# Spreading the softmax reciprocals by transfers through DRAM instead of widened transposes, in a two-layer graph network kernel on one core

## The chip, the cores and the metric

The kernel runs on one core of one Trainium2 chip. The metric is the device time of one execution in microseconds, as a median of runs. The engines of the core are TensorE (PE, with its weight loads as PEld), VectorE (DVE), ScalarE (ACT), GpSimd (POOL) and SyncE (SP); each works through its own list of instructions in order, and semaphores connect them.

## The reference

Sixteen graphs of 512 nodes with 512 features go through two layers. The first picks one of four expert matrices for each graph, multiplies by the adjacency matrix and applies a batch normalisation and a ReLU; the second, which the change touches, is an attention with 16 heads of 32 columns and the adjacency matrix as a bias:

```python
x = _layernorm(x + L0(x, adj, ...))
a = jnp.einsum('bhnd,bhmd->bhnm', q, k) * scale + (adj + adj)[:, None]
row_nonzero = jnp.any(a != 0, axis=-1, keepdims=True)
a = jnp.where(row_nonzero, a, -jnp.inf)
p = jax.nn.softmax(a, axis=-1)
p = jnp.where(jnp.isnan(p), 0.0, p)
o = jnp.einsum('bhnm,bhmd->bhnd', p, v)          # B=16, H=16 heads, N=512, hd=32
x = _layernorm(x + o.transpose(0, 2, 1, 3).reshape(B, N, D) @ Wo.T)
```

All of it is float32. Large products are made of three products of rounded high and low parts.

## The kernel before, in words

Layer 0 runs first, over all 16 graphs; layer 1 follows, from about 400 us on, and is written out for every batch `b` (one graph). A batch has 16 steps `s`. Four steps make a group `g` of four heads; step `s` handles rows `t = s % 4` (128 of them) of the four heads of group `s // 4`. Each engine has its own order of the work of a step, written out by hand in its function `batch`, and the batches overlap: the projections of the next batch and the output projection of the one before fill the slots between the attention steps.

In step `s` PE makes the scores of step `s+1` (`scores`, line 630, four heads), one dense slot of 12 matmuls (line 615, from the list `SLOTS`), the transposes of the probabilities of step `s` (`prob_transpose`, line 661), and in every second step the products of the transposed probabilities with `v` (`weigh_v`, line 645). DVE adds the bias to the scores and takes row maxima (`bias_and_max`, line 1175), ACT takes the exponential with its row sum (`exp`, line 881) and copies the transposed probabilities out of PSUM (`copy_probT`, line 781; the fourth head is copied by DVE in most steps, line 1189).

When a group's four steps are through, its 16 x 128 row sums have to divide the product. The result of a group lies in `pv_bank` with partition = head and column, free dimension = row n, while the row sums lie with the row n on the partition. So in the last step of a group, DVE forms `inv_sum` and `zeros_inv` (`inverse_sum`), POOL subtracts them and repeats each value 32 times (`recip_wide`, [128, 16, 32], line 479), and in the first step of the next group (`s % 4 == 0`) PE transposes the four 128 x 128 blocks of it (`spread_recip`, line 653) into `t_bank[0]`. ACT copies the bank to `recip` (`copy_recip`), DVE multiplies `pv_bank` by it (`weigh`, line 1205, the last or nearly the last thing that DVE does in that step, waiting for `r_sb` and `pv_ps`), and ACT and DVE split the result into its high and low parts (`oT_high`, `oT_low`) at the steps in `OT_STEPS`: group 0 in step 6, group 1 in step 8, group 2 in step 12, group 3 in step 0 of the next batch. For groups 1, 2 and 3 that is the very step of the `weigh`. On ACT, `oT_high` stands after the first two `copy_probT` and ahead of the exponentials of the next step.

POOL also forms the reciprocal standard deviations of both layer norms (`layer_norm_rstd`), stores the outputs (`store_out`, line 486) and loads the next batch's x (`load_x`, line 494) over the tile of z that a store has freed. SP issues all else: above all `pack`, which moves the staged q and k into the layout of the scores, 1 MB for each slot of kind k or q (line 386), the adjacency rows (line 371), layer 0's output (line 375) and the copies of x1 to DRAM and back.

Of the kernel before, what the change touches and what calls it, by code (L numbers as in the profile page):

```python
# [41 lines left out]
         + [("o", 0, -1), ("o", 1, -1), ("o", 2, -1), ("q", 2, 0), ("o", 3, -1), ("k", 3, 0), ("q", 3, 0)]  # L42
# [5 lines left out]
X_LOADS = {2: 0, 4: 1, 5: 2, 6: 3}  # L48
# [7 lines left out]
OT_STEPS = {0: 3, 6: 0, 8: 1, 12: 2}  # L56
# [47 lines left out]
def gnn_program(nc, x, adj, adj_t, router_wt, router_b, expert_w, bn_gamma, bn_beta, WqT, WkT, WvT, WoT, out):  # L104
    outT_dram = nc.dram_tensor("outT_spill", [B, H, N], F32).ap()
    x1_dram = nc.dram_tensor("x1_spill", [B, N, H], F32).ap()

# [8 lines left out]
    with ExitStack() as ctx:  # L116
# [56 lines left out]
        with ExitStack() as l1:  # L173
# [12 lines left out]
            recip_wide = sb(l1, "recip_wide", [P, NT * J, HD])  # L186
# [81 lines left out]
        r_sb = sem("r_sb")  # L268
        o_norm = sem("o_norm")
# [162 lines left out]
        def _(pool):  # L432
# [29 lines left out]
            def softmax_weights(b, g):  # L462
# [15 lines left out]
                wide = [P, NT * J, HD]  # L478
                nc.gpsimd.tensor_tensor(recip_wide[:, :, :],
                                        inv_sum[:, :].rearrange("p (a o) -> p a o", o=1).broadcast_to(wide),  # L480
                                        zeros_inv[:, :].rearrange("p (a o) -> p a o", o=1).broadcast_to(wide),
                                        ALU.subtract).then_inc(wide_done, 1)

# [18 lines left out]
            def batch(b, par, first, last):  # L502
                for s in range(STEPS):
                    if s in X_LOADS and not last:
                        load_x(b + 1, X_LOADS[s], first)
# [9 lines left out]
            iterations(batch)  # L515
            for t in range(NT):
                layer_norm_rstd(1, B - 1, t, f_mv, f_eps, f_rstd)
# [5 lines left out]
        def _(pe):  # L523
# [125 lines left out]
            def spread_recip(b, g):  # L649

                pe.wait_ge(wide_done, G * b + g + 1)
                for t in range(NT):
                    ins = nc.tensor.transpose(t_bank[0][:, t * P:(t + 1) * P],  # L653
                                              recip_wide[:, J * t:J * t + J, :].rearrange("p a d -> p (a d)"),
                                              ident[:, :])
                ins.then_inc(r_ps, 1)
# [122 lines left out]
        def _(act):  # L779
# [109 lines left out]
            def copy_recip(b, g):  # L889
                act.wait_ge(r_ps, G * b + g + 1)  # L890
                need(act, oT_lo, G * b + g)
                copy(recip[:, :], t_bank[0][:, :]).then_inc(r_sb, 1)
# [17 lines left out]
            def batch(b, par, first, last):  # L910
                for s in range(STEPS):
# [6 lines left out]
                    if s in XT_EARLY and not last:  # L918
                        xT_high(b + 1, XT_EARLY[s], xT_bank[XT_EARLY[s]])
                    copy_probT(b, s, 0)  # L920
                    copy_probT(b, s, 1)
                    if s in OT_STEPS and not (first and s == 0):
                        oT_high(b if s else b - 1, OT_STEPS[s])
# [411 lines left out]
```

## Time and profile before

| | before |
|---|---|
| median of 3 runs | 2219.53 us (2218.31 to 2220.68) |
| profiled execution | 2221.48 us, its span 2219.7 us |
| PE busy | 2126.9 us, 96% of the span |
| DVE busy | 1584.6 us, 71% |
| ACT busy | 1567.1 us, 71% |
| POOL busy | 302.7 us, 14% |
| mean granted clock of PE | 0.989 |
| moved by DMA | 297.18 MB, 134 GB/s over the span |

Busy times are of one profiled execution. PE counts as busy while a matmul is in its pipeline; issuing a DMA, waiting and branching are not counted. A timeline row gives the start, the duration, the engine, the line and operation, what is written from what, how many were merged, and in brackets the idle time ahead of it with the instruction that ended it. The layers' two parts look different: layer 1 repeats every 110.8 us, one batch, which is the distance of the `weigh_v` rows of step 12 in successive batches (1301.26 us and 1412.06 us in the chain of work that ended last).

### The profile page before, as it was taken

The page shows a single profiled execution, that of the slowest core. Times are in us where ns is not written, and L with a number is a line of the kernel's source. Part 1 is how long each engine was busy: PE and PEld are TensorE (multiplying, and loading weights), DVE is VectorE, ACT ScalarE, POOL GpSimd, SP SyncE. Part 2 cuts the span into 40 slices and gives each one's busy share as a digit, 9 for nine tenths or more (in the row PEclk, how much of TensorE's full clock was granted, in tenths as well). Part 3 has the DMA queues.
Part 4 walks back from the last instruction along what each step waited for, and adds up shares of the span by engine and source line. Part 5 has one row for each costly group of instructions (what it writes and reads, how often), then busy time and mean ns, then how long its engine had stood idle before and what let it go on. Part 6 is the DMA issues. An engine that isn't in the chain of part 4 may idle for free.

```text
span 2219.7 us, 42446 instructions
## 1 busy us (share of the span) xinstructions
PE 2126.9 (96%) x14627; PEld 1685.1 (76%) x14627; DVE 1584.6 (71%) x4020; ACT 1567.1 (71%) x3501; POOL 302.7 (14%) x659
## 2 busy tenths in 40 slices
PE   6999999689999999999999999999999999999996
PEld 5778887467777777777777777777777777777774
DVE  5887877366768686868686868686868686868675
ACT  3544443287878787878787878787878787878784
POOL 0000000110202020202020202020202020202011
PEclk9999999799999999999999999999999999999999
DMA  6444342687777777777777777777778777877761
GB/s 225 158 162 155 124 159 85 121 143 129 138 133 134 134 135 132 136 130 138 135 132 134 134 134 134 132 136 130 135 132 136 134 134 130 136 134 133 132 100 45
DMA packets 149008, 297.18 MB, mean 134 GB/s; under 512 B 14514, under 2 KB 14546, under 8 KB 148690
## 3 DMA queue, kind: packets, MB, share of 16 engines
q1 hardware_dynamic: 137490, 256.97, 61.7%
q0 software_dynamic: 11328, 37.76, 6.1%
q8 instruction: 110, 1.80, 0.4%
q14 instruction: 80, 0.66, 0.1%
HBM read 110.12 MB, written 50.33 MB: 72 GB/s over the span
## 4 chain that ended last, share of the span: by engine, by line
PE 71%; issue 13%; DVE 7%; ACT 7%; DMA 1%; POOL 0%; SPq 0%; DVEq 0%; ACTq 0%; POOLq 0%
PE bank L615 27%; PE bank L661 18%; PE bank L645 11%; PE bank L630 8%; ACT prob L881 3%; DVE prob L1175 3%; PE bank L535 2%; ACT probT L781 2%; PE bank L552 2%; PE bank L587 1%; PE bank L653 1%; DVE z L1140 1%; DVE st_ln L1133 1%; DVE probT L1189 1%; DMA qp<-stage_q 1%
## 5 line engine op out<-in xcount | busy, mean ns | idle before, releaser
L1175 DVE CUSTOM_DVE_ANT_0 prob<-bank,adj_sb 128x512 f32<-128x512 f32 x1024 | 657.6, 685 | 141.0 <-PE bank L630 141.0
L881 ACT ACTIVATE prob<-prob,neg_max 128x512 f32<-128x512 f32 x1024 | 731.4, 723 | 9.4 <-DVE neg_max L1184 5.5
L781 ACT ACTIVATE probT<-bank 128x512 f32<-128x512 f32 x824 | 455.6, 594 | 321.1 <-PE bank L661 318.7
L661 PEld LDWEIGHTS bank<-ident,prob 128*128 128x128 f32 x4096 | 463.8, 140 | 110.6 <-issue 51.9
L661 PE MATMUL bank<-ident,prob 128*128 128x128 f32 x4096 | 541.0, 275 | 4.6 <-ACT probT L781 3.1
L630 PE MATMUL bank<-kp,qp 128*128 128x512 f32 x1024 | 347.3, 420 | 24.7 <-DVE row_max L1175 23.5
L1189 DVE COPY probT<-bank 128x512 f32<-128x512 f32 x200 | 136.4, 685 | 232.4 <-PE bank L661 232.4
L645 PE MATMUL bank<-probT,v 128*32 128x256 f32 x4096 | 247.6, 382 | 0.8 <-issue 0.8
L630 PEld LDWEIGHTS bank<-kp,qp 128*128 128x128 f32 x1024 | 175.9, 189 | 57.7 <-DVE row_max L1175 35.7
L615 PE MATMUL bank<-xT,wkT 128*128 128x512 f32 x768 | 205.3, 404 | 1.5 <-DVE xT L954 1.5
L881 ACT ACTIVATION_READ_ACCUMULATOR prob<-prob,neg_max 128x1 f32 x1024 | 204.4, 200 | 0.0
L615 PE MATMUL bank<-woT,oT 128*128 128x512 f32 x768 | 202.0, 399 | 0.0
L615 PE MATMUL bank<-xT,wqT 128*128 128x512 f32 x768 | 201.7, 398 | 0.0
L645 PEld LDWEIGHTS bank<-probT,v 128*32 128x32 f32 x4096 | 120.3, 109 | 104.3 <-issue 38.7
L535 PE MATMUL bank<-adjT,x_part 128*128 128x512 f32 x768 | 184.7, 397 | 13.1 <-DVE adjT L967 13.1
L615 PE MATMUL bank<-wvT,xT 128*128 128x512 f32 x768 | 196.2, 398 | 0.0
L552 PE MATMUL bank<-zT,w_sel 128*128 128x512 f32 x768 | 180.4, 393 | 8.4 <-ACT outT L781 5.2
L535 PEld LDWEIGHTS bank<-adjT,x_part 128*128 128x128 f32 x768 | 145.1, 191 | 43.7 <-issue 13.1
L552 PEld LDWEIGHTS bank<-zT,w_sel 128*128 128x128 f32 x768 | 144.7, 189 | 41.7 <-ACT outT L781 7.3
L615 PEld LDWEIGHTS bank<-xT,wkT 128*128 128x128 f32 x768 | 142.0, 192 | 29.7 <-issue 1.9
L615 PEld LDWEIGHTS bank<-woT,oT 128*128 128x128 f32 x768 | 139.4, 188 | 27.9 <-DVE oT L954 0.4
L615 PEld LDWEIGHTS bank<-wvT,xT 128*128 128x128 f32 x768 | 139.7, 188 | 27.5
(112 smaller groups left out, 2091.5 us busy)
## 6 DMA issues: line engine op xcount, KB each, us to landing
kp<-stage_k SPq DMA_DIRECT2D x256, 256.0 KB, 6.9
qp<-stage_q SPq DMA_DIRECT2D x256, 256.0 KB, 8.5
x_raw<-in_x_dram SPq DMA_DIRECT2D x16, 1024.0 KB, 7.5
adj_raw<-in_adj_t_dram SPq DMA_DIRECT2D x16, 1024.0 KB, 9.6
outT_spill<-outT SPq DMA_DIRECT2D x16, 1024.0 KB, 5.1
v<-outT_spill SPq DMA_DIRECT2D x16, 1024.0 KB, 15.1
z<-in_x_dram POOLq DMA_DIRECT2D x64, 256.0 KB, 3.9
adj_sb<-in_adj_dram SPq DMA_DIRECT2D x64, 256.0 KB, 8.2
```

Of the source, the lines that this page charges most:

```text
L535: ins = mm(z_bank[i][:, :], x_part[a][:, mt, i * P:(i + 1) * P], adjT[c][:, mt, :], start=(mt == 0 and n == 0), stop=(mt == NT - 1 and n = ...
L552: ins = mm(ps[:, :], w_sel[a][:, ht, i * P:(i + 1) * P], zT[c][:, ht, :], start=(ht == 0 and n == 0), stop=(ht == NT - 1 and n == 2))
L587: ins = nc.tensor.transpose(ps[:, kt * P:(kt + 1) * P], v[:, par, kt, t * P:(t + 1) * P], ident[:, :])
L615: ins = mm(ps[:, :], w, m, start=(t == 0 and n == 0), stop=(t == NT - 1 and n == 2))
L630: mm(s_bank[j][:, :], qp[:, g % 2, j, t * P:(t + 1) * P], kp[:, g % 2, j, :], start=True, stop=True).then_inc(s_ps, 1)
L645: ins = mm(pv_bank[j * HD:(j + 1) * HD, (t - 1) * P:(t + 1) * P], v[:, par, mt, c:c + HD], probT[:, j, mt, :], start=(mt == 0), stop=(mt = ...
L653: ins = nc.tensor.transpose(t_bank[0][:, t * P:(t + 1) * P], recip_wide[:, J * t:J * t + J, :].rearrange("p a d -> p (a d)"), ident[:, :])
L661: ins = nc.tensor.transpose(t_bank[j % 2][:, mt * P:(mt + 1) * P], prob[:, s % 2, j, mt * P:(mt + 1) * P], ident[:, :])
L781: return nc.scalar.activation(dst, src, ACT.Copy, scale=scale)
L881: nc.scalar.activation(prob[:, s % 2, j, :], prob[:, s % 2, j, :], ACT.Exp, scale=2.0, bias=neg_max[:, s % 2, j:j + 1], accum_out=row_sum[ ...
L1175: nc.vector.tensor_tensor_reduce(prob[:, s % 2, j, :], s_bank[j][:, :], adj_sb[:, t, :], 1.0, LOWEST, ALU.add, ALU.max, row_max[:, g % 2, ...
L1189: nc.vector.tensor_copy(probT[:, j, :, s % 2 * P:(s % 2 + 1) * P], by_block(t_bank[j % 2])).then_inc(pT_dve, 1)
```

## The change

The widened transposes go. POOL subtracts only the 16 columns (`inv_live`, [128, 16]), PE transposes them with one instruction to [16, 128], ACT copies these 16 rows to `recip_rows`, and a new function `spread_rows` on the POOL queue stores them to a scratch tensor in DRAM (8 KB), waits for that to land, and loads for each of the four heads one row of 512 values into 32 partitions of `recip` (64 KB each). `weigh` now waits for these four loads in place of ACT's copy. `spread_rows` stands first in POOL's steps 0, 4, 8 and 12. The high and low parts of group 3 move from step 0 to step 1 of the next batch; to suit that, the slots of the output projection move one later (2, 3, 4, 5 instead of 1, 2, 3, 5) and the q slot of group 2 from 4 to 1; the x loads of tiles 1 to 3 move from steps 4, 5, 6 to 5, 6, 7.

```diff
 SLOTS = ([("k", 2, 0)]
-         + [("o", 0, -1), ("o", 1, -1), ("o", 2, -1), ("q", 2, 0), ("o", 3, -1), ("k", 3, 0), ("q", 3, 0)]
+         + [("q", 2, 0), ("o", 0, -1), ("o", 1, -1), ("o", 2, -1), ("o", 3, -1), ("k", 3, 0), ("q", 3, 0)]
-X_LOADS = {2: 0, 4: 1, 5: 2, 6: 3}
+X_LOADS = {2: 0, 5: 1, 6: 2, 7: 3}
-OT_STEPS = {0: 3, 6: 0, 8: 1, 12: 2}
+OT_STEPS = {6: 0, 8: 1, 12: 2}
+OT_LAST = 1
+    recip_dram = nc.dram_tensor("recip_spill", [B * G, J, N], F32).ap()
-            recip_wide = sb(l1, "recip_wide", [P, NT * J, HD])
+            inv_live = sb(l1, "inv_live", [P, NT * J])
+            recip_rows = sb(l1, "recip_rows", [NT * J, P])
...
-                nc.gpsimd.tensor_tensor(recip_wide[:, :, :],
-                                        inv_sum[:, :].rearrange("p (a o) -> p a o", o=1).broadcast_to(wide),
-                                        zeros_inv[:, :].rearrange("p (a o) -> p a o", o=1).broadcast_to(wide),
+                nc.gpsimd.tensor_tensor(inv_live[:, :], inv_sum[:, :], zeros_inv[:, :],
                                         ALU.subtract).then_inc(wide_done, 1)
+            def spread_rows(b, g):
+                n = G * b + g
+                pool.wait_ge(r_sb, n + 1)
+                pool.dma_start(recip_dram[n:n + 1, :, :].rearrange("o j (t n) -> t (o j) n", n=P),
+                               recip_rows[:, :]).then_inc(recip_out, 16)
+                need(pool, oT_lo, n)
+                pool.wait_ge(recip_out, 16 * n + 16)
+                for j in range(J):
+                    pool.dma_start(recip[j * HD:(j + 1) * HD, :],
+                                   recip_dram[n:n + 1, j, :].broadcast_to([HD, N])).then_inc(recip_in, 16)
...
                 for s in range(STEPS):
+                    if s % NT == 0 and s > 0:
+                        spread_rows(b, s // NT - 1)
+                    elif s == 0 and not first:
+                        spread_rows(b - 1, G - 1)
                     if s in X_LOADS and not last:
...
-                for t in range(NT):
-                    ins = nc.tensor.transpose(t_bank[0][:, t * P:(t + 1) * P],
-                                              recip_wide[:, J * t:J * t + J, :].rearrange("p a d -> p (a d)"),
-                                              ident[:, :])
-                ins.then_inc(r_ps, 1)
+                nc.tensor.transpose(t_bank[0][0:NT * J, 0:P], inv_live[:, :], ident[:, :]).then_inc(r_ps, 1)
...
-                need(act, oT_lo, G * b + g)
-                copy(recip[:, :], t_bank[0][:, :]).then_inc(r_sb, 1)
+                need(act, recip_out, 16 * (G * b + g))
+                copy(recip_rows[:, :], t_bank[0][0:NT * J, 0:P]).then_inc(r_sb, 1)
...
+                    if s == OT_LAST and not first:
+                        oT_high(b - 1, G - 1)
                     copy_probT(b, s, 0)
                     copy_probT(b, s, 1)
-                    if s in OT_STEPS and not (first and s == 0):
-                        oT_high(b if s else b - 1, OT_STEPS[s])
+                    if s in OT_STEPS:
+                        oT_high(b, OT_STEPS[s])
...
-                dve.wait_ge(r_sb, G * b + g + 1)
+                dve.wait_ge(recip_in, 64 * (G * b + g + 1))
                 dve.wait_ge(pv_ps, 8 * b + 2 * g + 2)
                 tt(recip[:, :], pv_bank[:, :], recip[:, :], ALU.mult).then_inc(o_norm, 1)
...
                         bias_and_max(nb, ns, (0, 1, 2))
+                    if s == OT_LAST and not first:
+                        oT_low(b - 1, G - 1)
...
                         weigh(gb, gg)
-                    if s == 0 and not first:
-                        oT_low(b - 1, OT_STEPS[s])
```

## Rows read from the trace of the kernel before

**Rows 1.** The page: busy time of PE, and the chain's shares by engine
```profile
PE 2126.9 (96%) x14627; PEld 1685.1 (76%) x14627; DVE 1584.6 (71%) x4020; ACT 1567.1 (71%) x3501; POOL 302.7 (14%) x659
...
PE 71%; issue 13%; DVE 7%; ACT 7%; DMA 1%; POOL 0%; SPq 0%; DVEq 0%; ACTq 0%; POOLq 0%
```

**Rows 2.** Windows: stretch: length, busy us by engine, granted clock, DMA share, GB/s
```profile
1299.70:1306.30 6.60, 6.60 (x64) 4.90 (x64) 3.46 (x11) 4.19 (x11) 0.00 (x0) 1.00 0.94 128
...
1325.00:1332.50 7.50, 7.50 (x68) 5.66 (x67) 5.03 (x13) 5.37 (x13) 0.46 (x1) 1.00 1.08 184
...
1352.00:1358.70 6.70, 6.70 (x65) 5.01 (x64) 5.04 (x14) 5.10 (x12) 3.92 (x8) 1.00 0.23 78
...
1378.80:1389.00 10.20, 9.20 (x79) 6.94 (x78) 8.91 (x21) 6.83 (x16) 3.02 (x6) 1.00 1.08 156
```

**Rows 3.** Timeline of step 12 of one batch, from the transposes on
```profile
1300.20 0.59 PEld L653 LDWEIGHTS bank<-ident,recip_wide 128*128 128x128 f32 x4
...
1301.06 0.60 ACT L781 ACTIVATE recip<-bank 128x512 f32<-128x512 f32 x1 [0.32 <-PE bank L653]
...
1303.27 0.69 DVE L1205 TENSOR_TENSOR recip<-bank,recip 128x512 f32<-128x512 f32 x1 [0.76 <-PE bank L645]
...
1304.72 0.63 ACT L781 ACTIVATE oT<-recip 128x512 fp32r<-128x512 f32 x1
...
1306.65 0.59 ACT L781 ACTIVATE probT<-bank 128x512 f32<-128x512 f32 x1
...
1308.58 1.03 PE L661 MATMUL bank<-ident,prob 128*128 128x128 f32 x8
```

**Rows 4.** Timeline of steps 0 and 1 of the next batch
```profile
1327.24 0.60 ACT L781 ACTIVATE recip<-bank 128x512 f32<-128x512 f32 x1
...
1332.64 0.69 DVE L1189 COPY probT<-bank 128x512 f32<-128x512 f32 x1 [0.38 <-PE bank L661]
...
1333.25 0.68 DVE L1175 CUSTOM_DVE_ANT_0 prob<-bank,adj_sb 128x512 f32<-128x512 f32 x1
...
1334.52 0.39 PE L630 MATMUL bank<-kp,qp 128*128 128x512 f32 x1
```

**Rows 5.** Timeline of steps 4 and 5 of that batch
```profile
1353.92 0.59 ACT L781 ACTIVATE recip<-bank 128x512 f32<-128x512 f32 x1
...
1359.17 0.69 DVE L1175 CUSTOM_DVE_ANT_0 prob<-bank,adj_sb 128x512 f32<-128x512 f32 x1 [2.04 <-PE bank L630]
...
1360.69 0.39 PE L630 MATMUL bank<-kp,qp 128*128 128x512 f32 x1
```

**Rows 6.** Timeline of steps 8 and 9 of that batch
```profile
1380.95 0.59 ACT L781 ACTIVATE recip<-bank 128x512 f32<-128x512 f32 x1
...
1385.68 0.68 DVE L1148 TENSOR_TENSOR z<-bank,z 128x512 f32<-128x512 f32 x1
...
1389.49 0.69 DVE L1175 CUSTOM_DVE_ANT_0 prob<-bank,adj_sb 128x512 f32<-128x512 f32 x1 [1.61 <-PE bank L630]
...
1390.24 0.50 PE L630 MATMUL bank<-kp,qp 128*128 128x512 f32 x1
```

**Rows 7.** Groups of POOL: the widening, and the issue of a 256 KB store
```profile
L479 POOL TENSOR_TENSOR recip_wide<-inv_sum,zeros_inv 128x512 f32<-128x512 f32 x64 | 72.2, 1129 | 110.0 <-issue 96.6 <-POOL live L473 12.9 <-DVE zeros_inv L1199 0.5
L486 POOL DMA_DIRECT2D out_dram<-z x64 | 39.1, 612 | 36.8 <-DVE z L1140 34.5 <-issue 2.2
```

**Rows 8.** Issue to landing, POOL queue: all stores of 256 KB (line 486)
```profile
DMA to landing us min/median/max: 2.4/3.2/9.6
```

**Rows 9.** The same: loads of 256 KB (line 494), all; the one at 1324.8 us
```profile
DMA to landing us min/median/max: 2.8/4.2/11.6
...
DMA to landing us min/median/max: 8.1/8.1/8.1
```

**Rows 10.** Windows of the first layer and of the start of layer 1
```profile
30.00:35.00 5.00, 2.66 (x8) 2.13 (x9) 5.00 (x3) 3.92 (x3) 0.00 (x0) 0.84 0.00 0
...
440.00:445.00 5.00, 2.79 (x7) 2.03 (x8) 4.41 (x15) 2.10 (x6) 0.00 (x0) 0.80 1.09 129
```

More of the change, by code:

```diff
@@ L268, in gnn_program @@
         r_sb = sem("r_sb")
+        recip_out = sem("recip_out")
+        recip_in = sem("recip_in")
         o_norm = sem("o_norm")
@@ L477, in softmax_weights @@
                 wait_apart(pool, r_ps, G * b + g)
-                wide = [P, NT * J, HD]
-                nc.gpsimd.tensor_tensor(recip_wide[:, :, :],
-                                        inv_sum[:, :].rearrange("p (a o) -> p a o", o=1).broadcast_to(wide),
-                                        zeros_inv[:, :].rearrange("p (a o) -> p a o", o=1).broadcast_to(wide),
+                nc.gpsimd.tensor_tensor(inv_live[:, :], inv_sum[:, :], zeros_inv[:, :],
                                         ALU.subtract).then_inc(wide_done, 1)
+            def spread_rows(b, g):
[8 more added lines that the diff above has]
+                                   recip_dram[n:n + 1, j, :].broadcast_to([HD, N])).then_inc(recip_in, 16)
             def store_out(b, t):
@@ L515, in _ @@
             iterations(batch)
+            spread_rows(B - 1, G - 1)
             for t in range(NT):
```

## The prediction

> **What bounds the kernel now.** I read the page first, then windows over one batch of layer 1, then the timeline around each of its four hand-overs of the reciprocals, and last how long the POOL queue's transfers take. The page shows PE busy 96% of the span and 71% of the chain on PE [rows 1]. In windows around three of the four hand-overs PE is busy for the whole stretch, and for 9.20 of 10.20 us in the fourth, at a granted clock of 1.00 [rows 2]. So PE sets the pace, nearly without gaps: a microsecond taken off PE comes off the time, and any wait that PE meets for longer than the slack of the engine that feeds it goes on top. The other column to see is the DMA share: 0.94 in step 12, 1.08 in step 0, 1.08 in step 8, but 0.23 in step 4. Three of the four places where the change wants a fast transfer have full DMA engines.
>
> **What is taken away.** PE loses three of four transposes. Four weight loads, which pace them, take 0.59 us [rows 3], so three are 0.44 us; 64 groups give 28 us, all on PE's path. The remaining transpose has only 16 columns of weights and can only be cheaper. ACT's copy of 128x512 (0.60 us) becomes one of 16x128, for which I take 0.25 us (no row shows it; it is between nothing and 0.6 us); ACT isn't the bound there, and the gain is counted below as an earlier start. POOL's 1.13 us becomes a 16-column subtraction, at most as long [rows 7]; POOL is 14% busy and works ahead, so it is worth nothing.
>
> **What is added: a round trip T** from the end of the small copy to the landing of the last of the four loads, ahead of DVE's `weigh`. It is one store, its landing, four issues in a row and the last one's landing. An issue holds POOL 0.61 us [rows 7]; I take 0.6. From issue to landing a 256 KB store takes 2.4 us at best [rows 8] and a 256 KB load 2.8 us [rows 9]. With these T = 2.4 + 3 x 0.6 + 2.8 = 7.0 us on idle DMA engines. The transfers here are smaller (8 KB, and 64 KB four times), which takes off some of the data's part; five issues alone are 3.0 us, which is the floor. I take 6.3, nearer to the 7.0 since most of a short transfer's landing doesn't look like data. On full engines the load issued at 1324.8 us took 8.1 us [rows 9] and the slowest store 9.6 us [rows 8]: T could be up to 9.6 + 1.8 + 8.1 = 19.5 us. The new transfers have fewer packets to be held up, so I stay near the low end: 8.5 us in steps 0 and 12, 7.5 in step 8, 6.3 in step 4.
>
> The Trainium skill (DMA: Bandwidth & Descriptors, Anatomy of one DMA — SWDGE (gpsimd) path) fits such a transfer as about 2.0 us plus its bytes at 436 GB/s. For 256 KB that estimate is 2.6 us, and the best rows, 2.4 and 2.8, agree. For this change it would give 2.0 + 1.8 + 2.15 = 6.0 us in an estimate, which is the second rival's value, at every group.
>
> **What T costs, group by group.** What waits is in-order, so everything behind it shifts.
> Step 12: the small copy ends at about 1301.0 (the old one began at 1301.06 after a wait of 0.32 for the four transposes). `weigh` would end at 1301.7 + T; it takes 0.69. Behind it in the same step waits ACT's `oT_high`, which began at 1304.72, and behind that on ACT are two exponentials and the copy of the third head's transposed probabilities, 1306.65 to 1307.24. PE wants that bank for the transposes recorded at 1308.58, loading weights from about 1308.35: 1.1 us of slack. PE's wait is T - 3.0 - 1.1 = T - 4.1 [rows 3]; at 8.5, 4.4 us.
> Step 0: the copy ends at 1327.5, `weigh` at 1328.2 + T. Here `oT_high` has been moved to step 1, so ACT doesn't wait at once; but DVE does, and its next work began at 1332.64, then the maxima at 1333.25, which end 0.5 us ahead of the scores at 1334.52 that need their bank. PE's wait is T - 4.4 - 0.5 = T - 4.9 [rows 4]; at 8.5, 3.6 us.
> Step 4: copy until 1354.2, `weigh` until 1354.9 + T; DVE's next work was at 1359.17 after 2.04 us of idling, 0.8 us ahead of PE's need at 1360.69. PE's wait is T - 5.1 [rows 5]; at 6.3, 1.2 us.
> Step 8: copy until 1381.2, `weigh` until 1381.9 + T; next on DVE is the sum for the next batch's x at 1385.68, its statistics and a copy, then 1.61 us idle, then the maximum at 1389.49, for which PE's scores at 1390.24 wait without slack. PE's wait is T - 3.8 - 1.6 = T - 5.4 [rows 6]; at 7.5, 2.1 us. `oT_high` stands in this step too, and gives a little less.
> The wait on DVE and the one on ACT run side by side, so the larger counts. Steps 4, 8 and 12 come 16 times and step 0 15 times: 16 x (1.2 + 2.1 + 4.4) + 15 x 3.6 = 123 + 54 = 177 us. At the very end the last `weigh` stands bare, but PE has other output products; I put 4 us.
>
> **Edits that I cost at nothing.** The slots are exchanged, not added: PE has 12 matmuls in each either way. DVE's work for the output projection (sum and statistics, about 1.6 us) leaves step 2 and comes to step 5, where DVE is loaded; the idle time at steps 5 to 8 is what hides it, and if `weigh` has used that up it is 0.9 us more in each batch, 14 us. The x loads are one step later, each behind a store issued one step later; `spread_rows` also holds POOL for T less the last landing, some 4 to 6 us, ahead of the stores, the layer norm's rstd and the loads. The loads are wanted at the end of steps 6 to 8, 10 us after their issue, against 4.2 us in the median and 11.6 at worst [rows 9]. The group-3 parts are one step later and so are the slots that read them. Of the DMA bytes, 264 KB are added to each group.
>
> **The sum**, against the profiled execution's 2221.5 us: 2221.5 - 28 + 177 + 4 = 2374.5 us. It is 2 us above the median of the runs, so I forecast 2373 us.
>
> **Rivals.**
> *The round trip is hidden (faster).* If T stays under the 4.1 to 5.4 us of slack at every group, only the 28 us are left: 2192 us. That needs each landing within about 1.2 us after its issue ends (5.3 less five issues, halved). For it: no transfer as small as these stands in the trace. Against it: 2.4 us is the minimum of 64 stores. It turns at a mean wait of 0.44 us, T of about 5.3. Chance 0.08 for a gain, 0.03 for a draw.
> *Traffic doesn't matter, T is about 6 everywhere.* The waits are 1.9, 1.1, 0.9 and 0.6 us: 16 x 3.4 + 15 x 1.1 + 3 - 28 = +46 us, 2266 us. For it: an engine may take turns between queues packet by packet, and these transfers give each only one or two packets at a time. The Trainium skill (DMA: Bandwidth & Descriptors, Queues, rings and completion order) says that it does so. Against it: the 8.1 us load in a full stretch has eight packets an engine and yet 5.3 us more than the quickest. Chance 0.24.
> *Worse in traffic, or the clock falls.* With T of 12 in steps 0 and 12 and 10 in step 8 the waits are 7.9, 7.1, 4.6 and 1.2: +302 us, 2521 us. Besides, where PE was busy for only 2.66 and 2.79 of 5 us the granted clock was 0.84 and 0.80 [rows 10], that is part of the stretch at the lower of the levels 2.4 and 1.2 GHz; 0.20 of 5 us is 1 us for each long wait, 31 of them, 31 us on any of the cases. Chance 0.20.
> *The x chain.* If store and load are both slow (over 15 us in all), the sum for x at steps 6 to 8 waits on DVE; 2 to 3 us in a batch, 40 us more on the forecast. Chance 0.05, inside the range.
>
> **Numbers.** The forecast has 0.40, its worse neighbours 0.25, the 6 us case 0.24, the hidden case 0.11. The range leaves out the gain and the draw and most of what lies over T = 12: 2235 to 2500 us. A measurement of this kernel tells 0.2%, about 4 us, from no change. Faster 0.08, same 0.03, slower 0.89.
>
> **What would show it.** In the profile after: idle time of DVE ahead of line 1205's `weigh` put down to a DMA of `recip`, several microseconds each, where it idled 0.76 us by PE in step 12 [rows 3]; one transpose in place of four; POOL issues at 0.6 us; PE idle ahead of scores or transposes in steps 1, 5, 9 and 13; the landing of the four loads shorter in step 4 than in steps 0 and 12. The forecast is wrong if the round trip is under 5.3 us, or if ACT and DVE win back in the steps between what they lose; it is then PE's share of the chain that stays above 70%.

## The result and the profile after

| | before | after |
|---|---|---|
| median | 2219.56 us | 2848.95 us (2842.78 to 2849.55, 4 runs) |
| ratio | | 1.283, 95% interval 1.281 to 1.284 |
| span of the profiled execution | 2219.7 us | 2846.9 us |
| PE busy / not busy in the span | 2126.9 / 92.8 us | 2268.8 / 578.1 us |
| mean granted clock | 0.989 | 0.893 |

Slower, as forecast, but by 629 us where 153 were forecast. The page of the kernel after, in the form of [rows 1]: busy time, granted clock in tenths along the span, the chain by engine and by line.

```profile
PE 2268.8 (80%) x14435; PEld 1780.7 (63%) x14435; DVE 1583.1 (56%) x4020; ACT 1553.1 (55%) x3501; POOL 425.7 (15%) x979
...
PEclk9999989889898988888998888888989888889888
...
PE 37%; DMA 24%; issue 14%; DVE 10%; ACT 10%; POOL 4%; SPq 0%; DVEq 0%; POOLq 0%; ACTq 0%
DMA recip_spill<-recip_rows 16%; PE bank L634 13%; PE bank L676 10%; DMA recip<-recip_spill 7%; ACT prob L896 5%; DVE prob L1192 4%; PE bank L649 4%; PE bank L664 4%; POOL recip L495 3%; ACT probT L796 2%; PE bank L554 2%; PE bank L571 1%; DVE st_ln L1150 1%; ACT v L870 1%; PE bank L606 1%
```

PE's share of the chain fell from 71% to 37%, and a transfer of 8 KB (`recip_spill`) now holds 16% of it, more than any matmul line. Who waited for whom (total, times, longest, in us):

```profile
DVE recip L1222 <- DMA recip<-recip_spill: 669.7, 64, 16.2
...
ACT oT L796 <- DVE recip L1222: 451.0, 48, 14.6
POOL recip L495 <- DMA recip_spill<-recip_rows: 444.4, 64, 10.4
...
PE bank L649 <- DVE row_max L1192: 389.7, 86, 15.0
```

That is the chain that the prediction named: POOL waits for its store, DVE's `weigh` for the loads, ACT's `oT_high` for `weigh`, PE's scores for DVE. The timeline of step 0 of one batch, the place of [rows 4]:

```profile
1630.98 0.25 ACT L796 ACTIVATE recip_rows<-bank 16x128 f32<-16x128 f32 x1
...
1631.52 0.63 POOL L490 DMA_DIRECT2D recip_spill<-recip_rows  x1 [3.58 <-ACT recip_rows L796]
...
1641.24 1.97 POOL L495 DMA_DIRECT2D recip<-recip_spill  x4 [9.09 <-DMA recip_spill<-recip_rows]
...
1647.51 0.69 DVE L1222 TENSOR_TENSOR recip<-bank,recip 128x512 f32<-128x512 f32 x1 [14.95 <-DMA recip<-recip_spill]
...
1649.46 0.80 PE L649 MATMUL bank<-kp,qp 128*128 128x512 f32 x1 [11.23 <-DVE row_max L1192]
```

The round trip T, from the end of the small copy (1631.23) to the start of `weigh`, is 16.3 us: 0.3 until POOL issues, 9.2 until the store of 8 KB has landed, 0.5 until the first load is issued, 1.5 for three more issues, and 4.8 for the last landing. PE waits 11.23 us for scores. Times from issue to landing over the whole execution, first the 64 stores of 8 KB, then the 256 loads of 64 KB (min, median, max), as in [rows 8, 9]:

```profile
DMA to landing us min/median/max: 1.8/6.0/10.5
...
DMA to landing us min/median/max: 2.1/2.5/6.1
```

Taken from the timeline as above for the inner 14 batches, the medians of T in steps 4, 8, 12 and 0 are 10.2, 14.0, 10.5 and 16.4 us. Between one group's small copy and the next PE idles 5.1, 9.9, 6.0 and 11.3 us, as means over all groups; the last batch's step 8 alone has 17.4 us, and without it the 9.9 are 9.4. (The kernel before idles 1.3 us in step 4 and next to nothing in the others.) The forecast had 1.2, 2.1, 4.4 and 3.6 us: it is 1.4 times too short in step 12 and three to five times in the others.

The last two stores of the execution, where SP has no packs in flight, took 1.8 us each. The other 62 were issued while transfers of SP were under way. Each landed between 0.4 us before and 1.5 us after the last one of SP's that had been issued ahead of it (medians 1.1, 0.5, 0.4 and 0.4 us after it, in the order of the steps). So the store of 8 KB comes in as if it stood in line behind them. Part of the delay passes before its data move: the first of its packets starts 5.9 us after the issue in step 0 and 2.7 us in steps 4 and 12 (medians), 1.3 us in the quiet store.

The clock, in windows of 10 us around the end of two such waits (PE had idled 11.2 us until 1649.46 and 7.9 us until 1570.04; length, busy us of PE, PEld, DVE, ACT, POOL, granted clock, DMA share, GB/s), to be set beside the 1.00 of [rows 2]:

```profile
1646.00:1656.00 10.00, 6.54 (x31) 5.73 (x32) 6.20 (x16) 5.14 (x11) 0.00 (x0) 0.68 0.08 21
1569.00:1579.00 10.00, 7.95 (x33) 7.04 (x34) 8.17 (x19) 8.37 (x20) 0.79 (x2) 0.58 0.27 101
```

A mean of 0.58 between the levels 1.0 (2.4 GHz) and 0.5 (1.2 GHz) is most of 10 us at the lower level. Over the whole span the granted clock is at 0.5 for 607 us, mostly 6.8 to 13.7 us at a time around the waits, and PE is busy in 346 us of them; in the kernel before it is 50 us, PE busy in 24.

**Where the time went.** The span grew by 627.2 us: 485.3 of PE not busy and 141.9 of PE busy. PE has 28 us less to do, so its matmuls took some 170 us more, 2.7 us a group. That is what the clock explains: half of the 346 us that PE was busy at the lower level is 173 us, 12 us in the kernel before. Both parts come from the same 64 waits.

### The profile page after: what moved, and what is told of

It reads as the page before. It is cut to its first block, busy times and chain, and to the rows that moved or that the text cites. A ratio compares the mean times of both kernels' runs of the same rounds, so it can differ in the third digit from the quotient of the medians.

```text
span 2846.9 us, 42445 instructions
## 1 busy us (share of the span) xinstructions
PE 2268.8 (80%) x14435; PEld 1780.7 (63%) x14435; DVE 1583.1 (56%) x4020; ACT 1553.1 (55%) x3501; POOL 425.7 (15%) x979
## 4 chain that ended last, share of the span: by engine, by line
PE 37%; DMA 24%; issue 14%; DVE 10%; ACT 10%; POOL 4%; SPq 0%; DVEq 0%; POOLq 0%; ACTq 0%
DMA recip_spill<-recip_rows 16%; PE bank L634 13%; PE bank L676 10%; DMA recip<-recip_spill 7%; ACT prob L896 5%; DVE prob L1192 4%; PE bank L649 4%; PE bank L664 4%; POOL recip L495 3%; ACT probT L796 2%; PE bank L554 2%; PE bank L571 1%; DVE st_ln L1150 1%; ACT v L870 1%; PE bank L606 1%
## 5 line engine op out<-in xcount | busy, mean ns | idle before, releaser
L649 PE MATMUL bank<-kp,qp 128*128 128x512 f32 x1024 | 371.0, 444 | 390.5 <-DVE row_max L1192 389.7
L676 PE MATMUL bank<-ident,prob 128*128 128x128 f32 x4096 | 613.0, 299 | 12.1 <-ACT probT L796 11.7
L676 PEld LDWEIGHTS bank<-ident,prob 128*128 128x128 f32 x4096 | 531.4, 155 | 126.8 <-issue 65.4
L1222 DVE TENSOR_TENSOR recip<-bank,recip 128x512 f32<-128x512 f32 x64 | 44.2, 691 | 669.7 <-DMA recip<-recip_spill 669.7
L796 ACT ACTIVATE oT<-recip 128x512 fp32r<-128x512 f32 x64 | 40.3, 630 | 451.0 <-DVE recip L1222 451.0
L634 PE MATMUL bank<-woT,oT 128*128 128x512 f32 x768 | 217.0, 421 | 4.1 <-DVE oT L971 4.1
L634 PE MATMUL bank<-xT,wqT 128*128 128x512 f32 x768 | 217.4, 422 | 0.0
L634 PE MATMUL bank<-wvT,xT 128*128 128x512 f32 x768 | 215.0, 426 | 0.0
L495 POOL DMA_DIRECT2D recip<-recip_spill x256 | 127.1, 503 | 451.9 <-DMA recip_spill<-recip_rows 444.4
L554 PE MATMUL bank<-adjT,x_part 128*128 128x512 f32 x768 | 183.3, 395 | 13.7 <-DVE adjT L984 13.7
L634 PEld LDWEIGHTS bank<-wvT,xT 128*128 128x128 f32 x768 | 153.0, 207 | 30.6
## 6 DMA issues: line engine op xcount, KB each, us to landing
v<-outT_spill SPq DMA_DIRECT2D x16, 1024.0 KB, 13.6
```

What stands on the lines that cost most here:

```text
L495: pool.dma_start(recip[j * HD:(j + 1) * HD, :], recip_dram[n:n + 1, j, :].broadcast_to([HD, N])).then_inc(recip_in, 16)
L554: ins = mm(z_bank[i][:, :], x_part[a][:, mt, i * P:(i + 1) * P], adjT[c][:, mt, :], start=(mt == 0 and n == 0), stop=(mt == NT - 1 and n = ...
L634: ins = mm(ps[:, :], w, m, start=(t == 0 and n == 0), stop=(t == NT - 1 and n == 2))
L649: mm(s_bank[j][:, :], qp[:, g % 2, j, t * P:(t + 1) * P], kp[:, g % 2, j, :], start=True, stop=True).then_inc(s_ps, 1)
L676: ins = nc.tensor.transpose(t_bank[j % 2][:, mt * P:(mt + 1) * P], prob[:, s % 2, j, mt * P:(mt + 1) * P], ident[:, :])
L796: return nc.scalar.activation(dst, src, ACT.Copy, scale=scale)
```

## The experiments

All are against the kernel before on the same chip, which took 2219.6 to 2221.3 us each time. Where T and idle times are given by step, they are medians (T) and means over all groups (idle) read from the timeline as above, in the order 4, 8, 12, 0.

**1. The moves alone.** The kernel before with the changed lists and the later high and low parts of group 3, on the old path by four transposes.

```diff
-         + [("o", 0, -1), ("o", 1, -1), ("o", 2, -1), ("q", 2, 0), ("o", 3, -1), ("k", 3, 0), ("q", 3, 0)]
+         + [("q", 2, 0), ("o", 0, -1), ("o", 1, -1), ("o", 2, -1), ("o", 3, -1), ("k", 3, 0), ("q", 3, 0)]
-X_LOADS = {2: 0, 4: 1, 5: 2, 6: 3}
-OT_STEPS = {0: 3, 6: 0, 8: 1, 12: 2}
+X_LOADS = {2: 0, 5: 1, 6: 2, 7: 3}
+OT_STEPS = {6: 0, 8: 1, 12: 2}
+OT_LAST = 1
...
```

> The kernel before with the moves alone: the q slot of group 2 to slot 1, the output projection to slots 2 to 5, the x loads of tiles 1 to 3 to steps 5 to 7, the high and low parts of group 3 to step 1. The reciprocals still go by four transposes. My theory (the moves are worth next to nothing, all of the loss is the new round trip and what follows from it): 2220 us, within 15 us. Rival (the moves take DVE's and POOL's slack in steps 5 to 8 and are a good part of the 629 us): 2300 us or more, with idle time of PE ahead of the transposes or scores of steps 5 to 9.

Measured: 2227.5 us, ratio 1.0032 (1.0018 to 1.0046). The moves cost 7 us; the other 622 are the path of the reciprocals.

**2. Stale rows: loads that needn't wait for the store.**

```diff
-                pool.wait_ge(recip_out, 16 * n + 16)
+                old = max(n - 1, 0)
+                pool.wait_ge(recip_out, 16 * old + 16)
                 for j in range(J):
                     pool.dma_start(recip[j * HD:(j + 1) * HD, :],
-                                   recip_dram[n:n + 1, j, :].broadcast_to([HD, N])).then_inc(recip_in, 16)
+                                   recip_dram[old:old + 1, j, :].broadcast_to([HD, N])).then_inc(recip_in, 16)
```

> The changed kernel, but the four loads read the rows of the group before in DRAM (so the reciprocals are those of another group) and so needn't wait for this group's store to land; everything else, the store too, stays. Theory 1 (what is slow is a write to DRAM and its receipt, 5 to 10 us of each round trip, and loads on the same queue aren't held up): the round trip is 0.65 + 1.5 + 2.2 to 4.8 us, 4.4 to 7 us; PE's waits nearly go and the time is 2250 to 2350 us. Theory 2 (a short transfer of any kind issued while SP's pack transfers are in flight waits behind them): the loads land as late as store and loads did before less 2 us, 7 to 11 us after their issue in steps 0 and 8, and the time stays over 2600 us.

Measured: 2730.3 us, ratio 1.230. The loads' landings and DVE's wait:

```profile
DMA to landing us min/median/max: 2.1/7.5/12.2
...
DVE recip L1223 <- DMA recip<-recip_spill: 546.9, 64, 13.2
```

The same loads that took 2.5 us in the median now take 7.5: the waiting that the store had done ahead of them they do themselves. So it isn't only the write to DRAM that is slow; loads issued into the same traffic wait as long. T is 6.5, 12.2, 10.7 and 13.4 us.

**3. Thin packs.** From the third group on, each of SP's pack transfers moves 32 of 128 rows (the scores use stale rows).

```diff
-                        sp.dma_start(f32(dst[part * HD:(part + 1) * HD, ring, :, :]).rearrange("p j n -> p (j n)"),
-                                     f32(stage[m][half][:, :])).then_inc(packed[m], 16)
+                        rows_moved = HD if b == 0 and g < 2 else HD // 4
+                        sp.dma_start(f32(dst[part * HD:part * HD + rows_moved, ring, :, :]).rearrange("p j n -> p (j n)"),
+                                     f32(stage[m][half][0:J * rows_moved, :])).then_inc(packed[m], 16)
```

> The changed kernel, but from the third group on each of SP's q and k pack transfers moves 32 of its 128 rows (64 KB in place of 256 KB; the scores use stale rows). Same count of transfers. Theory 1 (a store to DRAM is slow by itself): the stores land as before, median 6 us, up to 10 us; the time stays within 10% of 2849 us. Theory 2 (the wait is behind the pack transfers): the stores land in 1.8 to 3 us and the loads in 2.1 to 2.5 us, the round trip is about 6 us, and the time falls to 2250 to 2400 us. The last two stores of the changed kernel, with no pack beside them, landed in 1.8 us.

Measured: 2506.2 us, ratio 1.129; the stores', then the loads' landings, and DVE's wait:

```profile
DMA to landing us min/median/max: 1.7/2.5/4.2
...
DMA to landing us min/median/max: 2.1/2.2/4.4
...
DVE recip L1223 <- DMA recip<-recip_spill: 360.5, 64, 8.8
```

Taking bytes away from another queue brings the 8 KB store from 6.0 to 2.5 us. T is 6.2, 8.2, 7.1 and 9.5 us. The time was 106 us over the upper end expected: even this T is beyond the slack in every step, and PE not busy is 300.0 us (2510.2 span less 2210.2 busy), 207 over before, with 111 us of slow matmuls on top (2210.2 less 2126.9, plus 28).

**4. The same thin packs in the kernel before,** a control.

> A control: the kernel before with the thin packs (32 of 128 rows from the third group on). Both theories want it to be at 2215 to 2222 us, since PE doesn't wait for packs there. If it is much faster, part of what thin packs gained in the changed kernel was not the round trip.

Measured: 2217.5 us, ratio 0.9988 (0.9978 to 0.9998). So the 343 us that thin packs gave the changed kernel came by way of its round trips.

**5. The store issued by ACT.**

```diff
-                pool.dma_start(recip_dram[n:n + 1, :, :].rearrange("o j (t n) -> t (o j) n", n=P),
-                               recip_rows[:, :]).then_inc(recip_out, 16)
...
+                n = G * b + g
...
+                act.wait_ge(r_sb, n + 1)
+                act.dma_start(recip_dram[n:n + 1, :, :].rearrange("o j (t n) -> t (o j) n", n=P),
+                              recip_rows[:, :]).then_inc(recip_out, 16)
```

> The changed kernel, but the 8 KB store is issued by ACT right behind its small copy; the loads stay on POOL. Theory 1 (the POOL queue is what is slow: issue in software and a queue of its own behind its other transfers): the store lands in about 2.5 us, the time falls to 2500 us or less. Theory 2 (the DMA engines behind are shared and full of SP's packs): landing still 4 to 9 us and the time within 5% of 2849 us.

Measured: 2814.2 us, ratio 1.268. T is 8.8, 13.6, 10.5 and 16.0 us, shorter by 1.4 us at most. So it isn't the POOL queue that is slow; the traffic met the store on ACT's queue too.

**6. No trip to DRAM: rows straight from SBUF.**

```diff
-                pool.dma_start(recip_dram[n:n + 1, :, :].rearrange("o j (t n) -> t (o j) n", n=P),
-                               recip_rows[:, :]).then_inc(recip_out, 16)
-                pool.wait_ge(recip_out, 16 * n + 16)
...
-                    pool.dma_start(recip[j * HD:(j + 1) * HD, :],
-                                   recip_dram[n:n + 1, j, :].broadcast_to([HD, N])).then_inc(recip_in, 16)
+                    rows4 = recip_rows[J * j:J * j + J, :].rearrange("p (o n) -> p o n", o=1)
+                    pool.dma_start(recip[:, j * P:(j + 1) * P],
+                                   rows4.broadcast_to([J, HD, P])).then_inc(recip_in, 16)
...
```

> The changed kernel without the trip to DRAM: the four DMAs on the POOL queue take the 16 rows straight from SBUF (each four rows of 512 B, repeated over 32 partitions each), so the store and its landing are gone. Theory 1 (each transfer issued beside SP's packs waits behind them once, whatever it is): the round trip loses the quiet part of the store, about 2.5 us, and in each group keeps the wait behind the packs; with a mean of 12.7 us before, 9 to 10 us are left, and the time is 2600 to 2730 us, near the kernel with stale rows (2730 us). Theory 2 (the DRAM write is slow in itself): the round trip is 4 to 6 us and the time under 2350 us.

Measured: 2815.3 us, ratio 1.268: neither of the two. The landings of the four transfers:

```profile
DMA to landing us min/median/max: 2.7/8.6/14.0
```

T is 8.4, 15.0, 11.5 and 15.4 us. One of the two hops is gone, and T is shorter by 1.8 and 1.0 us in two steps and longer by 1.0 in the others. They now carry 512 B a packet, four times as many packets, and a longer issue (0.68 us for 0.50); which of it uses up the gain wasn't taken apart.

**7. Everything that waits, one step later** (rows by DRAM as in the change).

```diff
-OT_STEPS = {6: 0, 8: 1, 12: 2}
-OT_LAST = 1
+OT_STEPS = {6: 0, 10: 1, 13: 2}
+OT_LAST = 2
...
+                    late_end = None
+                    if s % NT == 1 and not (first and s == 1):
+                        late_end = (b, s // NT - 1) if s > 1 else (b - 1, G - 1)
...
-                    if group_end:
-                        weigh(gb, gg)
+                    if late_end:
+                        weigh(*late_end)
```

> The changed kernel with everything that waits for the round trip one step later: weigh in steps 1, 5, 9, 13 in place of 0, 4, 8, 12, the high and low parts of groups 1, 2 and 3 in steps 10, 13 and 2. That gives each group 6.8 us more slack, 10.9 to 12.2 us in all. My theory (PE waits for the round trip less the slack, 31 us a batch in the changed kernel): of the round trips of 16.3, 9.7, 15.1 and 11.0 us there are left 4.4, 0, 2.9 and 0.1 us a batch, some 7 us, 115 us in all, less 28 us saved, and some clock: 2300 to 2380 us. Rival (the engines are bound by something else that the change brought, such as POOL being held up or the added DMA traffic): over 2500 us.

Measured: 2498.0 us, ratio 1.125, between the two ranges. PE idles 0.8, 2.6, 6.0 and 5.4 us: 14.8 a batch for 32.3. Step 4 has no wait left. But the traffic's timing shifted with the rest, and T of step 12 grew from 10.5 to 16.4 us, so that step didn't gain; that is the miss. The store of step 12 still takes 4.9 us, the last of its loads 8.7 us where it had taken 3.3: in the batch looked at, two packs of slot 12 go out between the store's landing and the third load. So each hop pays for what goes out ahead of it.

**8. Both: rows from SBUF, and a step later.**

> Both: rows straight from SBUF, and everything that waits for them one step later. Round trip 9 to 10 us in the mean, 13 at most, against 10.9 to 12.2 us of slack. My theory: PE waits about 1 us a batch or less, the three transposes saved are 28 us, the moves cost 7: 2195 to 2230 us. Rival (more traffic and waits in POOL leave a part): 2250 to 2350 us.

Measured: 2380.6 us, ratio 1.070 (1.067 to 1.073), above both ranges. T is 14.8, 11.6 and 15.0 us in steps 8, 12 and 0, where 13 at most was expected, and PE idles 0.8, 2.7, 2.7 and 3.6 us.

**9. Three packs held back until the rows of a group have landed,** in the changed kernel, and (10) in the kernel of 8.

```diff
+HELD = {7: 1, 11: 2, 15: 3}
...
+                    if s in HELD and is_live(s, first, last):
+                        sp.wait_ge(recip_in, 64 * (G * b + HELD[s] + 1))
                     if kind in "kq" and is_live(s, first, last):
                         pack(kind, b + rel, i)
```

> The changed kernel with nothing but the three held packs. Its round trips are 14.0, 10.5 and 16.4 us in steps 8, 12 and 0. My theory: they fall to the 7 to 10 us seen with thin packs, step 4 stays at 10.2, and PE waits for each round trip less 4.1 to 5.4 us, 14 to 20 us a batch in place of 31: 2450 to 2600 us. Rival (not the packs issued just ahead but the queue as a whole): over 2750 us.

Measured: 2673.1 us, ratio 1.203. T is 11.0, 10.2, 6.4 and 7.5 us: in the three steps that were held it falls from 14.0, 10.5 and 16.4, in step 4, which wasn't, it doesn't (10.2 before). What is issued just ahead is what the short transfer waits behind. The time fell by 176 us only and ended 73 us above the range. Holding has a price of its own: ACT waits 41.6 us for `stage_q`, and PE 78.3 us in 15 waits for which the profile names no releaser ("issue"). In each of these 15 PE starts 0.1 us after the last pack of q slot 12 has landed, which SP had to issue behind the held one of slot 11.

> The kernel with the rows taken straight from SBUF and all that waits for them one step later, and besides SP holds back three pack transfers a batch until the loads of a group have landed: that of q slot 7 for group 1, of k slot 11 for group 2, of q slot 15 for group 3. So those 1 MB no longer lie ahead of the short transfers on the DMA engines. My theory (short transfers wait behind packs already issued): the round trips of steps 8, 12 and 0 fall from 14.8, 11.6 and 15.0 us to 7 to 10 us, less than the 11 to 12 us of slack; PE's waits go, and the time is 2195 to 2240 us. Rival (the held packs come late for the scores that need them, or the packs ahead of the held ones fill the engines all the same): round trips over 11 us in two of the steps, or PE waiting for a DMA of kp or qp, and 2300 us or more.

Measured: 2516.9 us, ratio 1.133, worse than 8 by 136 us. The rival held on the time and on the late packs. The theory held on the round trips: the last landing now comes 8.0, 7.7 and 7.8 us after the copy in steps 8, 12 and 0, where it had come at 14.7, 11.6 and 14.9. `weigh`'s wait is all but gone, and two others stand in its place:

```profile
DVE recip L1223 <- DMA recip<-recip_rows: 11.0, 3, 7.8
...
PE bank L650 <- issue: 141.9, 16, 9.7
...
ACT stage_q L797 <- DMA qp<-stage_q: 102.3, 16, 7.1
```

Slots 15 and 1 both stage through `stage_q`. And the packs of slot 12, behind the held one of slot 11, come late for the first scores of the next batch: PE starts 0.1 us after the last of them in all 16 waits.

**11. The packs moved out of the way in place of held.** From 8: k1, q1, v3 in slots 13 to 15, and only q slot 7 held.

```diff
-         + [("v", 0, 1), ("v", 1, 1), ("v", 2, 1), ("k", 0, 1), ("q", 0, 1), ("v", 3, 1), ("k", 1, 1), ("q", 1, 1)])
+         + [("v", 0, 1), ("v", 1, 1), ("v", 2, 1), ("k", 0, 1), ("q", 0, 1), ("k", 1, 1), ("q", 1, 1), ("v", 3, 1)])
...
+HELD = {7: 1}
```

> From the kernel with direct rows and late weigh: k1, q1, v3 take slots 13, 14, 15 in place of v3, k1, q1, so that q1's pack goes out one step earlier, 6.8 us ahead of the short transfers of step 0, and one pack is held (q slot 7, until group 1's rows are there); stage_q is free for its next user, 5 slots on. My theory (a round trip is the quiet 5 to 6 us plus what of the packs is still in flight, and PE waits for it less 11 to 12 us of slack): round trips of 12 us in step 8, 11.6 in step 12, 10 to 12 in step 0; PE idles 1 to 4 us a batch in all against 1.8 in the kernel before; with 28 us saved and 7 for the moves 2200 to 2250 us. Rival (the v load and adjacency loads fill the engines in step 0 as well as packs did, and held packs cost their own wait): the round trip of step 0 stays at 14 us or more, PE waits there 3 us or more, and the time is 2280 us or more.

Measured: 2350.5 us, ratio 1.058 (1.056 to 1.060), 30 us better than 8 and the fastest by this path, still 130 behind the kernel before. `weigh` in step 8 starts 12.0 us after the copy, which is where DVE comes to it, so nothing is waited for there; T of step 12 is 11.2 and of step 0 14.1 us: the rival's sign, in the stretch where 1 MB of v and the adjacency rows are loaded besides the packs; which of them sets it wasn't taken apart. PE idles 0.8, 1.6, 2.7 and 3.0 us. The span is 128 us longer than before: 104 us more of PE not busy (196.4 less 92.8) and 52 us of slow matmuls, less the 28.

**12 and 13. Needless matmuls in PE's waits,** to see what the clock is worth. First the dense slot twice more ahead of the step's last transposes:

> The changed kernel, but in the steps 0, 4, 8 and 12 PE makes the 12 matmuls of its dense slot two more times (same bank, same result), some 5 us of needless work a group, just ahead of where it waits. The changed kernel's PE is busy 142 us more than before though it has 28 us less to do, at a mean granted clock of 0.893 against 0.989. Theory 1 (the waits pull the clock down and slow matmuls are about 170 us of the 629): with PE busy most of the waits the granted clock is over 0.96 and the time falls by 60 to 150 us, to 2700 to 2790 us, though there is more to do. Theory 2 (the slow stretches lie beside work that sets nothing, and the waits alone are the loss): 2849 us or up to 100 us more.

Then behind them, 3, 1, 3 and 2 times in steps 0, 4, 8 and 12:

```diff
+AGAIN = {0: 3, 4: 1, 8: 3, 12: 2}
...
+                    if there and s in AGAIN:
+                        for n in range(AGAIN[s]):
+                            dense(kind, b + rel, i, range(NT), dense_bank[s % 2], n == AGAIN[s] - 1)
...
```

> The changed kernel with needless matmuls in PE's waits as in the other filled kernel, but put behind all transposes of the step, where nobody waits for them, and sized to the wait: the dense slot again 3, 1, 3 and 2 times in steps 0, 4, 8 and 12 (7.8, 2.6, 7.8 and 5.2 us at full clock, where PE waits 11.3, 5.1, 9.9 and 6.0 us). Theory 1 (the clock lost in the waits is about 170 us of slow matmuls, most of them on the path): granted clock over 0.96 and a time of 2700 to 2790 us. Theory 2 (slow matmuls mostly lie beside other waits): 2800 to 2880 us in spite of the clock.

Measured: 2820.2 us at a clock of 0.955, and 2821.1 us at 0.961, 29 and 28 us less than the changed kernel, with 1464 and 1656 more matmuls. The busy time of PE, first and second:

```profile
PE 2511.2 (89%) x15899; PEld 1980.1 (70%) x15899; DVE 1582.4 (56%) x4020; ACT 1553.1 (55%) x3501; POOL 426.7 (15%) x979
```

```profile
PE 2558.5 (91%) x16091; PEld 2015.9 (71%) x16091; DVE 1581.8 (56%) x4020; ACT 1550.8 (55%) x3501; POOL 426.0 (15%) x979
```

A matmul more costs about 0.23 us at full clock (a slot of 12 took 2.78 us in the chain of before). So at full clock PE would be busy 2126.9 - 28 + 337 = 2436 us and, with 381 in place of 337, 2480 us; 75 and 79 us of slow matmuls are left of 170. The granted clock agrees: PE was busy at the lower level for 145 and 148 us in place of 346. So over 90 us of slow matmuls are gone, and that gave 29 and 28 us of time. The round trips took little of it back: added up over the 64 groups, T grew by 18 and 5 us, mostly in step 0 (from 16.4 to 18.2 and 17.4 us).

So doing more work made the kernel faster, as the first theory has it, but by half of the least that it expected. The second filled kernel got the clock of the first theory (0.961) and the time of the second (2821 us). Most of the slow matmuls seem to lie beside other waits: over 90 us less of them were worth about 30 us. What all 170 would be worth stays open.

## Why the prediction was right and wrong

**Right: the chain, and what each step's slack is worth.** The prediction said that PE waits for T less 5.1, 5.4, 4.1 and 4.9 us in steps 4, 8, 12 and 0 [rows 3 to 6]. Put the measured T into it: 10.2 - 5.1 = 5.1, 14.0 - 5.4 = 8.6, 10.5 - 4.1 = 6.4, 16.4 - 4.9 = 11.5 us; measured were 5.1, 9.9 (9.4 without the last batch), 6.0 and 11.3 of idle time in all. Over the execution 16 x 20.1 + 15 x 11.5 = 494 us, against 485.3 us more than before. Single steps are off by up to about 1 us either way, so the sum's 2% is in part luck: 1.3 us of the idling in step 4 was there before. The kernel with everything a step later confirms it from the other side: 6.8 us more slack leaves 16.4 - 10.9 = 5.5 and 16.6 - 11.7 = 4.9 us in steps 12 and 0, and 6.0 and 5.4 were measured. With thin packs it is less exact: 179 us by the terms, 207 measured.

**Right: the parts of a quiet round trip.** 0.3 us to wake POOL, 1.8 for the store, 0.5 to the first issue, 1.5 for three issues, 2.2 for the last landing: 6.3 us, the value that I took for quiet engines. That it fits to the tenth is luck: the prediction had no term for the 0.8 us of waking up, and its landings and issues were too long by as much. The small copy took 0.25 us. The moves were costed at nothing with up to 14 us if DVE has no slack left; they cost 7.

**Wrong: the term T in traffic, the step "the new transfers have fewer packets to be held up, so I stay near the low end".** I took 6.3, 7.5, 8.5 and 8.5 us in steps 4, 8, 12 and 0, 30.8 a batch; measured were 10.2, 14.0, 10.5 and 16.4, 51.1 a batch. The rows had both ends (7.0 and 19.5 us) and the right end was named; the choice between them was argued from size, and being small didn't help: 8 KB waited 9.2 us where 256 KB had taken 8.1 [rows 9]. Thin packs, held packs, stale rows and the landings show what decides instead: a short transfer that is issued while transfers of SP are in flight lands late, and the store lands when the last of those ahead of it has landed. Loads and rows straight from SBUF are late too, but the fit is looser: by step, the medians lie from 3.2 us before that moment to 3.2 us after it. What is issued behind the store is quick (2.1 to 2.2 us in steps 4 and 8) only if nothing else has gone out in between; in steps 12 and 0 the last load took 3.3 and 4.8 us.

The kernel before had this on record, and it wasn't read: when ACT's old copy ended in steps 4, 8, 12 and 0, the last transfer of SP then in flight had 0, 7.8, 4.1 and 8.8 us still to go (medians). With 0.4 us more for the store and 4.2 for the handover, the issues and a quiet last landing that is an estimate of 12.4, 8.7 and 13.4 us for steps 8, 12 and 0. That is 1.6, 1.8 and 3.0 us short of the T measured, where the forecast was 6.5, 2.0 and 7.9 us short.

The second rival, that traffic doesn't matter, is refuted: 2.5 us of landing became 7.5 when the loads were issued into the traffic. It had leaned on a rule of the Trainium skill (DMA: Bandwidth & Descriptors, Queues, rings and completion order), that each engine takes turns between queues by the packet. Read as a promise for short transfers, that rule isn't borne out here: the store landed with the packs ahead of it. What goes on inside the engines no run here shows. The Trainium skill's formula (DMA: Bandwidth & Descriptors, Anatomy of one DMA — SWDGE (gpsimd) path), about 2.0 us plus the bytes at 436 GB/s, gives an estimate of 2.0 us for the store and 2.15 for a load. The quiet landings agree, with 1.8 and 2.2 us measured.

**Wrong in the same term: step 4 isn't quiet any more.** It was 0.23 of DMA share before [rows 2]; in the changed kernel the window around the round trip has 0.49, and the store took 5.1 us.

```profile
1519.30:1530.00 10.70, 6.54 (x55) 4.82 (x47) 2.96 (x9) 5.74 (x15) 4.05 (x8) 0.98 0.49 84
```

The packs of k slot 0 and q slot 1 go out at 1505.7 to 1510.8 us, 9 us ahead of it, and the last of them lands at 1524.4, the store at 1524.9. The kernel with the moves alone (1) shows that the moved q slot brought them there: at the end of ACT's copy in step 4 the last of these packs still had 3.6 us to go in the median, where the kernel before had none in flight.

**Wrong: the clock.** The third rival had the direction, but priced it from stretches with 2.3 us of idling [rows 10], at 1 us for each of 31 long waits. 61 of the waits of layer 1 were over 4 us, and the granted clock fell around every one of them: 5.4 us of PE's work a wait ran at half the clock, 170 us of slow matmuls in all. Filling the waits took over 90 us of these away and gave some 29 us of time.

**The sum again.** 2219.7 - 28 (transposes) + 485 (waits, 494 by the terms with the measured T) + 170 (slow matmuls) = 2847 us, the span after. The forecast had 177 + 4 for the waits and nothing for the clock, so in this account of PE's time about 304 of the 476 us that it missed stand under T and 170 under the clock. The account adds up by its making, since the span is PE's busy and idle time; it doesn't say that a full clock would give back 170 us. The range ended at 2500 because it took T = 12 in steps 0 and 12 and 10 in step 8 as the worst case, though the rows' own sum was 19.5.

**The hidden case** (faster, if T stays under the slack) didn't come, but the experiments say what it would need: T under 4 to 5 us where the quiet value is 6.3, or a step more of slack and packs out of the way in steps 8, 12 and 0. Packs out of the way in all three steps wasn't reached. The best of those tried was 5.8% slower than before. Not tried were a version with the loads of v and the adjacency rows moved as well, and one with a single transfer in place of four.

## What to carry to other kernels

A round trip through DMA in a busy kernel is priced by what the engines carry when it starts, not by its own bytes: read from the timeline when the last transfer issued ahead of it lands, and do so once for each hop. Compare the sum with the slack of each engine that waits in order behind it; here that subtraction gave PE's waits within 2% in the changed kernel and 14% too low with thin packs, once T was right. Where a formerly dense PE gets waits like the 4 to 12 us here, look for the slow clock around them as a term of its own, in windows around the end of a wait, and don't count all of it as time. Before you shift a transfer to another step, see which short transfer it will then stand ahead of.

## What the runs showed of the hardware that was not expected

- A store of 8 KB lands in 1.8 us alone and in up to 10.5 us with another queue's packs in flight, and then between 0.4 us before and 1.5 us after the last transfer issued ahead of it, in all 62 cases. Issued by ACT in place of POOL it is not much different (a round trip of 16.0 against 16.4 us).
- Part of the delay comes before its data move: in step 0 its first packet starts 5.9 us after the issue in the median, alone 1.3 us.
- Loads issued behind such a store took 2.2 us in the median of step 4, where nothing else had gone out, and 4.8 us in step 0. Without waiting for the store, the loads took 7.5 us.
- Issuing a short DMA from POOL takes 0.50 us with 2 KB rows, 0.68 us with four times as many 512 B rows.
- A PE that was given 1464 needless matmuls in its waits made the kernel 29 us faster.
